# Attention with 128-row score matmuls, the products with v moved by half a step, and three smaller moves at the end

## What is computed

```
h = layernorm(x);  q = h Wq^T + bq + ocr_bias;  k = h Wk^T + bk;  v = h Wv^T + bv
s = q k^T / sqrt(32) + band          # band: 0.1 where |i - j| <= 2
x = x + (softmax(s) v) Wo^T + bo
x = x + dequant(quant6(layernorm(x))) dequant(quant6(W))^T + bias
```

## Time and profile before

| | |
|---|---|
| median of 3 runs | 4154.99 us (4146.64 to 4157.97) |
| the profiled execution | 4162.25 us, its span 4160.4 us |
| busy share of the span | PE 97%, PEld 61%, DVE 81%, ACT 58%, POOL 73% |
| granted PE clock | 0.99 on average |
| projections | from 0 to 625 us |
| attention | from 625 to about 3735 us |
| last stage | from there to 4160 us |

### The profile page before, as it was taken

The page is one execution under the profiler, slowest core; times in us unless marked ns, Lnnn a source line. Parts: engine busy times, 40 slices in busy tenths (PEclk is TensorE's granted clock), DMA queues, the critical chain, the costliest instruction groups (busy, mean ns, idle before and its releaser), DMA issues.

```text
span 4160.4 us, 59566 instructions
## 1 busy us (share of the span) xinstructions
PE 4039.1 (97%) x21328; PEld 2537.2 (61%) x21328; DVE 3363.4 (81%) x5630; ACT 2407.6 (58%) x4651; POOL 3031.1 (73%) x1118
## 2 busy tenths in 40 slices
PE   8999999999999999999999999999999999987998
PEld 6788875555555555555555555555555555546877
DVE  6444568888888888888988888888888898867887
ACT  2122216766667667767676766776676767662332
POOL 2111108888988888889888888988888888974542
PEclk9999999999999999999999999999999999998999
DMA  7888759899999999999999999999999899986664
GB/s 246 264 265 255 231 158 180 182 213 189 200 199 193 200 192 205 188 211 185 210 185 212 189 199 200 194 200 192 203 188 208 181 212 185 210 193 170 178 168 102
DMA packets 292270, 825.16 MB, mean 198 GB/s; under 512 B 28832, under 2 KB 95392, under 8 KB 229536
## 3 DMA queue, kind: packets, MB, share of 16 engines
q0 software_dynamic: 72960, 486.57, 59.4%
q1 hardware_dynamic: 219040, 335.09, 28.9%
HBM read 211.82 MB, written 156.24 MB: 88 GB/s over the span
## 4 chain that ended last, share of the span: by engine, by line
PE 74%; DVE 15%; ACT 3%; POOL 3%; DMA 3%; issue 2%; SPq 0%; POOLq 0%; ACTq 0%; DVEq 0%
PE ps_a L872 19%; PE ps_a L858 19%; PE ps_b L837 16%; PE ps_p L481 12%; DVE part_max L1049 9%; PE ps_b L903 3%; DVE p_sb L1076 3%; POOL pair L1218 3%; PE ps_b L950 2%; ACT p_sb L1025 2%; PE ps_b L883 1%; DMA pair<-pair 1%; PE ps_a L933 1%; DMA k_odd<-wd_lo_d 1%; DMA q_st<-shift 0%
## 5 line engine op out<-in xcount | busy, mean ns | idle before, releaser
L1049 DVE TENSOR_REDUCE part_max<-ps_b 128x1 f32<-128x512 f32 x4016 | 2465.0, 680 | 375.5 <-PE ps_b L837 375.3
L1025 ACT ACTIVATE p_sb<-ps_a 128x512 f32<-128x512 f32 x4096 | 2083.6, 614 | 723.7 <-PE ps_a L858 719.5
L1218 POOL TENSOR_TENSOR pair<-p_sb 128x2048 f32<-128x2048 f32 x512 | 2454.1, 4813 | 65.7 <-ACT p_sb L1025 61.9
L872 PE MATMUL ps_a<-p_sb,v_sb 128*32 128x512 f32 x8192 | 995.8, 603 | 38.7 <-DVE p_sb L1076 21.9
L858 PE MATMUL ps_a<-q_st,k_odd 97*128 97x512 f32 x2048 | 843.9, 415 | 7.0 <-DMA q_st<-shift 3.8
L858 PE MATMUL ps_a<-q_st,k_even 97*128 97x512 f32 x2048 | 844.5, 412 | 5.3 <-PEq L163 3.8
L837 PE MATMUL ps_b<-k_odd,q_st 96*128 96x512 f32 x2048 | 813.2, 397 | 0.0
L837 PE MATMUL ps_b<-k_even,q_st 96*128 96x512 f32 x1968 | 783.0, 398 | 0.0
L858 PEld LDWEIGHTS ps_a<-q_st,k_odd 97*128 97x128 f32 x2048 | 387.6, 190 | 332.7 <-issue 214.3
L858 PEld LDWEIGHTS ps_a<-q_st,k_even 97*128 97x128 f32 x2048 | 387.7, 189 | 320.8 <-issue 219.4
L872 PEld LDWEIGHTS ps_a<-p_sb,v_sb 128*32 128x32 f32 x8192 | 224.4, 109 | 523.8 <-ACT p_sb L1025 319.9
(11 more groups left out here) (113 smaller groups left out, 2862.1 us busy)
## 6 DMA issues: line engine op xcount, KB each, us to landing
pair<-pair POOLq DMA_DIRECT2D x448, 1024.0 KB, 8.9
q_st<-q_hi_d SPq DMA_DIRECT2D x128, 256.0 KB, 7.1
xin<-in_x SPq DMA_DIRECT2D x16, 1024.0 KB, 8.7
xb_d<-xb SPq DMA_DIRECT2D x16, 1024.0 KB, 5.6
q_hi_d<-s_hi SPq DMA_DIRECT2D x64, 256.0 KB, 6.2
q_lo_d<-s_lo SPq DMA_DIRECT2D x64, 256.0 KB, 7.1
k_hi_d<-s_hi SPq DMA_DIRECT2D x64, 256.0 KB, 3.4
k_lo_d<-s_lo SPq DMA_DIRECT2D x64, 256.0 KB, 4.3
```

Source lines behind the costliest of these rows:

```text
L872: last = nc.tensor.matmul(ps_a[h * HD:(h + 1) * HD, RING_S, :], v_sb[:, kt, h * HD:(h + 1) * HD], p_sb[:, s % SLOTS, h, :], start=(kt == 0 ...
L1025: nc.scalar.activation(p_sb[:, s % SLOTS, h, :], ps_s[:, (HG * s + h) % RING_S, :], ACT.Exp, scale=SCALE).then_inc(p_ready, 1)
L1049: nc.vector.tensor_reduce(part_max[:, unit % 2, col, n:n + 1], ps_m[:, max_place(unit, j) % RING_M, :], AX.X, ALU.max).then_inc(max_taken, 1)
L1218: nc.gpsimd.tensor_tensor(pair[:, m % PAIR_RING], p_sb[:, s % SLOTS], p_sb[:, (s + 1) % SLOTS], ALU.add).then_inc(paired, 1)
```

## The change

1. `score` and `maximum` read all 128 rows. Rows 97 to 127 hold zeros on both sides: POOL clears rows 96 to 127 of q_st and k_even in the projections, and of k_odd in four parts after its adds 3, 5, 9 and 13. As `maximum` now reads row 96 too, q's must be zero then: SP copies a zero row over it after each load of q (`load_q`) from the fourth unit on.
2. The bursts stand before head 0 of even steps, for steps s - 4 and s - 3; those of the last two steps follow the loop. The key sums are in step 12, and ACT's copies move along (L984 to step 2, L989 to step 12, both before head 0).
3. wd_lo is loaded within the last unit (step 9), and wd_hi in step 6. For this wd_hi and wd_lo lie in parts 0 and 1 of k_odd, and o_lo of chunk 1 in part 2; DVE's `o_low(1)` waits for the scores of the first 12 steps.
4. The last chunk is stored in four parts, each when it is ready. In the chunk before it, DVE makes the residual sums after the quantising of the last chunk instead of between its steps.

```diff
@@ project, POOL
+            nc.gpsimd.memset(f32(q_st[ROWS:P]), 0.0).then_inc(ones_set, 1)
+            nc.gpsimd.memset(f32(k_even[ROWS:P]), 0.0).then_inc(ones_set, 1)
+            pool.wait_ge(ones_set, 2)
             nc.gpsimd.memset(f32(k_even[ROWS:ROWS + 1]), 1.0).then_inc(ones_set, 1)
@@ attend_and_finish
-    SUM_AT = 11
+    SUM_AT = 12
...
-    SUM_AFTER = HG * (SUM_AT + LEAD) + HG // 2
+    SUM_AFTER = HG * (SUM_AT + LEAD)
...
-        o_hi, o_lo = (k_even[:, 0], q_st[:, 1]), (q_st[:, 2], k_odd[:, 0])
-        wo_hi, wo_lo, wd_hi, wd_lo = k_even[:, 2], k_even[:, 3], k_odd[:, 1], k_odd[:, 2]
+        o_hi, o_lo = (k_even[:, 0], q_st[:, 1]), (q_st[:, 2], k_odd[:, 2])
+        wo_hi, wo_lo, wd_hi, wd_lo = k_even[:, 2], k_even[:, 3], k_odd[:, 0], k_odd[:, 1]
@@ SP
+                if unit >= RING_Q:
+                    sp.dma_start(f32(q_st[ROWS:ROWS + 1, i]), f32(q_st[ROWS + 1:ROWS + 2, i])).then_inc(q_loaded[i], 16)
...
-                    if unit == NU - 1 and kt == 9:
+                    if unit == NU - 1 and kt in (6, 9):
                         sp.wait_ge(scored, HG * (s - 1))
-                        sp.dma_start(f32(wd_hi), wd_hi_d).then_inc(wd_in, 16)
+                        n = (kt - 6) // 3
+                        sp.dma_start(f32((wd_hi, wd_lo)[n]), (wd_hi_d, wd_lo_d)[n]).then_inc(wd_in, 16)
...
-            sp.wait_ge(scored, HG * ST)
-            sp.dma_start(f32(wd_lo), wd_lo_d).then_inc(wd_in, 16)
@@ PE
-                nc.tensor.matmul(ps_m[:, bank, :], q_st[0:ROWS, unit % RING_Q, h, t * P:(t + 1) * P],
-                                 k_st[g % 2][0:ROWS, n, h, :], start=True, stop=True).then_inc(max_scored, 1)
+                nc.tensor.matmul(ps_m[:, bank, :], q_st[:, unit % RING_Q, h, t * P:(t + 1) * P],
+                                 k_st[g % 2][:, n, h, :], start=True, stop=True).then_inc(max_scored, 1)
...
             def burst(s):
-                if 3 <= s < ST + 3:
+                if s >= 4:
+                    weigh(s - 4)
                     weigh(s - 3)
-                    weigh(s - 2)
...
-            for s in range(ST + 2):
+            for s in range(ST + 1):
                 for h in range(HG):
-                    if s % 2 == 1 and h == HG // 2:
+                    if s % 2 == 0 and h == 0:
                         burst(s)
...
+            weigh(ST - 2)
+            weigh(ST - 1)
@@ ACT
-                    if h == HG // 2 and unit > 0:
-                        if kt == 1:
+                    if h == 0 and unit > 0:
+                        if kt == 2:
                             copy_o(unit - 1)
@@ DVE
                 if kt == 12:
+                    v.wait_ge(scored, HG * (KT * (NU - 1) + 3 * TT))
                     o_low(1)
...
-                    quantise(c + 1, lambda j: [last_sum(c, t) for t in ((0,), (1, 2), (3,))[j]])
+                    parts = ((0,), (1, 2), (3,)) if c + 2 < NCH else ((), (), (0, 1))
+                    quantise(c + 1, lambda j: [last_sum(c, t) for t in parts[j]])
@@ POOL
-            nc.gpsimd.memset(f32(k_odd[ROWS:ROWS + 1]), 1.0).then_inc(ones_set, 1)
...
+            def odd_rows(n):
+
+                nc.gpsimd.memset(f32(k_odd[ROWS:P, n]), 0.0).then_inc(ones_set, 1)
+                pool.wait_ge(ones_set, 3 + 2 * n + 1)
+                nc.gpsimd.memset(f32(k_odd[ROWS:ROWS + 1, n]), 1.0).then_inc(ones_set, 1)
+                pool.wait_ge(ones_set, 3 + 2 * n + 2)
...
+            for t in range(TT):
+                pool.wait_ge(res_ready, TT * c + t + 1)
+                pool.dma_start(out_ch[c][:, t, :], res[c % 2][:, t, :], accum_op=ALU.add).then_inc(out_done[c % 2], 16)
```

More of the change, by code:

```diff
@@ L494, in ahead @@
                     n_, h, t = j // (HG * TT), j // TT % HG, j % TT
+                    if place == 0:
+                        pe.wait_ge(ones_set, 3)
                     if j == 0:
@@ L498, in ahead @@
                         pe.wait_ge(k_loaded[n_], 48)
-                    nc.tensor.matmul(ps_t[:, place % RING_M, :], q_st[0:ROWS, unit, h, t * P:(t + 1) * P],
-                                     k_even[0:ROWS, n_, h, :], start=True, stop=True).then_inc(max_scored, 1)
+                    nc.tensor.matmul(ps_t[:, place % RING_M, :], q_st[:, unit, h, t * P:(t + 1) * P],
+                                     k_even[:, n_, h, :], start=True, stop=True).then_inc(max_scored, 1)
             pe.wait_ge(consts, 6)
@@ L811, in _ @@
                     store_rec(NG - 1)
-            for i in range(2):
-                sp.wait_ge(out_done[i], 16 * (NCH // 2))
+            sp.wait_ge(out_done[0], 16 * (NCH // 2))
+            sp.wait_ge(out_done[1], 16 * (NCH // 2 - 1 + TT))
             sp.wait_ge(o_out, 16 * NU)
@@ L832, in maximum @@
                 if j == 0:
-                    pe.wait_ge(q_loaded[unit % RING_Q], 48 * (unit // RING_Q + 1))
+                    pe.wait_ge(q_loaded[unit % RING_Q], 48 + 64 * (unit // RING_Q))
                 if u == 0 and j % (HG * TT) == 0:
+                    if g == 1:
+                        pe.wait_ge(ones_set, 3 + 2 * (n + 1))
                     pe.wait_ge(k_loaded[n], 48 * (g + 1))
                 bank = free_bank(max_place(unit, j))
-                nc.tensor.matmul(ps_m[:, bank, :], q_st[0:ROWS, unit % RING_Q, h, t * P:(t + 1) * P],
-                                 k_st[g % 2][0:ROWS, n, h, :], start=True, stop=True).then_inc(max_scored, 1)
+                nc.tensor.matmul(ps_m[:, bank, :], q_st[:, unit % RING_Q, h, t * P:(t + 1) * P],
+                                 k_st[g % 2][:, n, h, :], start=True, stop=True).then_inc(max_scored, 1)
             def turn(unit):
@@ L852, in score @@
                 unit, kt = s // KT, s % KT
-                if h == 0 and s == KT * QC:
-                    pe.wait_ge(ones_set, 2)
                 if h == 0 and kt == 0:
@@ L858, in score @@
                 nc.tensor.matmul(ps_s[:, (HG * s + h) % RING_S, :],
-                                 k_st[unit // QC % 2][0:ROWS + 1, kt // TT, h, kt % TT * P:(kt % TT + 1) * P],
-                                 q_st[0:ROWS + 1, unit % RING_Q, h, :], start=True, stop=True).then_inc(scored, 1)
+                                 k_st[unit // QC % 2][:, kt // TT, h, kt % TT * P:(kt % TT + 1) * P],
+                                 q_st[:, unit % RING_Q, h, :], start=True, stop=True).then_inc(scored, 1)
             def weigh(s):
@@ L1185, in _ @@
                     norm_factors(c + 1)
-                    quantise(c + 1, lambda j: [last_sum(c, t) for t in ((0,), (1, 2), (3,))[j]])
-                else:
+                    parts = ((0,), (1, 2), (3,)) if c + 2 < NCH else ((), (), (0, 1))
+                    quantise(c + 1, lambda j: [last_sum(c, t) for t in parts[j]])
+                else:
+                    for t in (2, 3):
+                        last_sum(c - 1, t)
                     for t in range(TT):
@@ L1224, in _ @@
                                    accum_op=ALU.add).then_inc(merged[n % CHAINS], 16)
+                if m in (3, 5, 9, 13):
+                    pool.wait_ge(paired, m + 1)
+                    odd_rows((3, 5, 9, 13).index(m))
                 if n == JOIN_AT and m > PAIRS:
@@ L1249, in _ @@
                     store(c - 3)
-            for c in range(NCH - 3, NCH):
+            for c in range(NCH - 3, NCH - 1):
                 store(c)
+            c = NCH - 1
+            for t in range(TT):
+                pool.wait_ge(res_ready, TT * c + t + 1)
+                pool.dma_start(out_ch[c][:, t, :], res[c % 2][:, t, :], accum_op=ALU.add).then_inc(out_done[c % 2], 16)
 def kernel(L0_attn_x, L0_attn_ocr_context, L0_attn_Wq, L0_attn_bq, L0_attn_Wk, L0_attn_bk, L0_attn_Wv,
```

5 lines of the change are left out of this document (2 added, 3 removed).

## The result

The changed kernel takes 4246.54 us (median; 4244.68 to 4251.29) against 4156.48 us, a ratio of 1.0217 with a 95% interval of 1.0202 to 1.0232: 90 us slower. Its profiled execution has a span of 4249.4 us against 4160.4, and the granted PE clock is 0.99 in both.

The account below looks back on a forecast made before the run. PE was taken as the bound, busy 97% of the span. Terms 108 (burst's place) - 12 + 8 - 4.5 - 5 - 2 - 4.5 = +88 us on 4155 gave 4243 us, range 4170 to 4310.

Parts of the forecast that it names:

- The bank's wait: Attention, pairs with large bands: PE's seventh and eighth maxima wait for DVE's takes, 1.17 us per pair, +146 us (112 to 175).
- the release: Attention, from the end of DVE's take to the matmul of the maximum that needs its bank: 0.12 + 0.21 = 0.33 us.
- The waits ahead of the bursts: Attention: `weigh` waits for its band until 0.94 us later, so PE's waits before bursts go, -38 us at most.
- 128 rows: Score and maximum matmuls: reading 128 rows instead of 97 and 96 may shorten their spacing, -12 us (0 to -26).
- The memsets: POOL's clearing: covered in the projections, but between its adds in the attention it costs +8 us (0 to 16).
- The small gains: PE's path: earlier shift, last scores no longer behind a burst, first burst waiting less for v, together -4.5 us.
- the earlier shift: Start of the last unit: maxima turned before a burst bring the shift 1.9 us earlier for the scores, -1.9 us.
- wd_lo: Last unit: loading it there removes PE's wait of 11.32 us, but chunk 2 is late next, -5 us (-2.7 to -11.3).
- The last two chunks: End of the kernel: PE's wait for DVE's quantising mostly goes, -2 us; storing in four parts, -4.5 us.
- The last store: End of the span: a quarter of the store lands in about 6.1 us, -4.5 us (-8 to 0).
- The banks don't bind: Rival, attention: the bands cost nothing at the banks and the waits ahead of bursts go, 4097 us; chance 0.15.
- Bands and adds collide more: Rival, attention: DVE's bands and POOL's adds exclude each other, 2 us more in each unit, 4367 us; chance 0.07.

## Why the prediction was right, step by step

Forecast 4243 us, measured 4246.5. The mechanism is the one forecast, and the experiments show it from three sides: moved alone the burst costs +99 us, one more take ahead of the bands only moves the wait, and without long bands it is gone. That the number came within 4 us is in part luck: one term was too large, and a piece that was not in the sum at all filled the gap. In units 4 to 61, with the sizes below and 116 pairs with large bands, 116 x 1.02 - 37 + 14 - 12 = +83 us, against 81.1 measured.

- **The bank's wait, +146 us (112 to 175): too large by an eighth.** Forecast were 1.17 us per pair. With the burst's move alone it is 6.82 - 5.80 = 1.02, so 125 x 1.02 = 127 us. (In the changed kernel it is 6.82 - 5.76 = 1.06, since its calm pairs gain by the 128 rows and those that DVE sets don't.) The step that was mis-sized is the release: from rows 4 I took 0.12 us to the weight load and 0.21 more to the matmul. After a real wait the row of the matmul begins with its weight load, both at 2231.22, 0.12 us after the take by the count of 0.61 us for one. The seventh maximum starts 5.80 us after the burst and in a calm pair 4.97, so it was 0.83 us late and not 1.03. The eighth comes 0.60 us behind it instead of 0.46, 0.14 more, as forecast, and the burst 0.1 later still.
- **Turn and key sums: missing.** With the burst before head 0 and the key sums in step 12, turn and sums fall between the same two bursts. Before they cost 0.10 and 0.85 us over a calm pair, together 0.95; now 6.95 - 5.76 = 1.19, and 8.17 - 6.95 = 1.22 with large bands instead of 1.06. Some 0.24 x 62 = 15 us, most of the 19 us by which the term above was too large. I counted eight maxima between bursts, but not that a turn takes a bank as the ninth: its weight load waits for a take in 62 units, 23.8 us in sum by the view of waits; before, when it stood in the middle of a pair, it had no wait.
- **The waits ahead of the bursts, -38 us: right in size.** In the kernel before, pairs with large bands had 6.19 us in the mean and calm ones 5.83, 0.36 x 87, and 0.2 us in 29 others: 37 us in 58 units. The bursts' waits for bands, 21.9 us by the view of waits, are all gone. The reason is probably only half the one given. The later burst gives a band more time, but bands are also no longer held up by adds, 96 overlaps down to 14. In the kernel before the 352 bands took 42 us more than their shortest times, in the changed one 13. That POOL's slack in the longer pairs is why was not tested alone; it fits the kernel with the bands behind the fourth take, which has the same order of PE, shorter pairs and 34 such overlaps.
- **128 rows, -12 us (0 to -26): right**, 12.2 us in 58 units. The Trainium skill ("TensorE: Matmul & The Clock Gate", LDWEIGHTS) was right about the weight load, 187 ns for 97 and for 128 rows. The zero that I drew from it was not, since the matmuls themselves follow each other at 233 ns instead of 235. The gain is real only where PE sets the pace: with the old bursts it went into collisions.
- **The memsets, +8 us (0 to 16): right in size.** Units 0 to 3 last 10.7 us longer than with the burst's move alone (212.7 against 202.0), and 12.8 us go when DMAs take the memsets' place. As forecast, the late adds hold up the slots of p: that made the first of the two long pairs in unit 1, +4.3 us. What I had not in the term is the other half, a band under a late add, +4.1 us in the second pair and 1.3 in one of unit 2.
- **The small gains, -4.5 us: not there.** The step that failed is the earlier shift (-1.9 us). The first score of the last unit waits for it longer than before, 8.0 us against 3.8. The shift was issued 15 us ahead of that score, at 3757.23, but took 14.9 us to land, where the median is 2.7 us; before, it took 8.7. Why it landed so late no run shows. The scores' row on the changed kernel's page:

```profile
L864 PE MATMUL ps_a<-q_st,k_odd 128*128 128x512 f32 x2048 | 840.3, 413 | 11.3 <-DMA q_st<-shift 8.0
```

  With that wait unit 62 is 4.2 us longer, while the last unit behind it lasts 51.3 us instead of 57.1: -1.6 together. From the last score to the first turn it takes 3.1 us more, which I had forecast as a gain of 1.7. Only the first burst's wait for v fell, from 4.0 to 2.1 us, a gain of 1.9 where I had taken 0.9.
- **wd_lo, -5 us: not confirmed.** The wait of 11.32 us is gone, and 7.4 us of what it gave came back in the linear steps: -4.5 us. But the time from the last score to the last turn is 405.1 us before and 403.6 now, 391.6 to 402.4 in the other kernels with wd_lo moved, and 398.3 and 400.1 in the two other kernels that leave it where it was. An effect of 5 us can't be told from that spread.
- **The last two chunks, -2 and -4.5 us.** The quantising wait fell from 2.67 to 1.13 us, -1.5 against -2. The last store gave 2.5 us, not 4.5: its four parts take 6.7 us each to land by the page of DMA issues, where I took 6.1, but two of them are issued together at 4241.54, 7.9 us before the end.

**The rivals.** *The banks don't bind* is excluded by the weight load of the seventh maximum, which waits 1.02 us for its take. *Bands and adds collide more* had the right rule and the wrong sign: overlaps fell. The exclusion that the Trainium skill ("SBUF — State Buffer", the two sides of SBUF) describes for a DVE operation with two SBUF inputs and GpSimd agrees with the band of 2.97 us above. By my reading it is why the two kernels with cut bands and the one with part 2 undone, in which calm pairs of PE are shorter than POOL's 6.02 us, came out 23 to 27 us slower than I expected.

## What to carry to other kernels

Where two engines share a ring of buffers, a side job of the consumer belongs where the consumer waits for the producer anyway. The same bands cost 1.06 us per pair behind the second or third take and 0.25 us behind the fourth or ahead of the first, and only the last place spares the turn and the bursts too. So count, for each place, which item of the ring is late, before moving the producer's long block; and ask of each engine that gets faster which exclusion it runs into next.

## What the runs showed of the hardware

- A DVE operation with both inputs in SBUF waits until a running POOL add has ended: a band of 128x8, 0.15 us alone, took 2.97 us and ended 0.04 us after the add.
- Matmuls of 128 rows follow each other 2 ns faster than those of 96 and 97 (233 against 235 ns from start to start; 397 against 400 ns for one), with equal weight loads of 187 ns. The 128-row matmuls in the projections had shown the same 0.233 us.
- Stored sums took 6.5 us until SP could issue the load that waits for them, at 1255.06 and 1261.52; what stood behind it on SP's queue, the shift, was 1.8 us late.
- A small DMA (the shift, 16 rows of 128) usually lands 2.7 us after its issue in the changed kernel (median of 64), but once took 14.9 us, at 3757.23.
